# One-core kernel of gated convolution and routed FFN: z is no longer transposed on TensorE in the convolution, the gates are computed in the FFN, and x's statistics come from two ScalarE passes

## The reference

```python
# convolution; c is the context, both keys and values
x = x + tanh(g_xattn) * conv_attention(k=c, v=c, q=layernorm(x))
#   kv[i, j] = k_i * v_j (8 x 8 products per head and batch); y = causal convolution of kv
#   with the head's filter of 1024 taps, plus D * kv; out_j = sum_i y[i, j] * q_i
z = layernorm(x)                     # 8192 tokens of 1024
# FFN
def ffn(t, w1, w2):                  # w1: 1024 x 1024, w2: 512 x 1024
    a, b = split(t @ w1, 2)
    return (a * silu(b)) @ w2
shared = ffn(z, shared_w1, shared_w2)
aff = sigmoid(z @ gate_w + expert_bias)                 # gate_w: 1024 x 7
mask = two best experts of each token
for e in range(7):
    sel = the 1170 tokens with the best where(mask, aff, -1) for e
    routed[sel] += ffn(z[sel], w1[e], w2[e]) * where(mask, aff, 0)
out = x + tanh(g_ffn) * (shared + routed)
```

## Time and profile before

| what | value |
|---|---|
| time, three runs | 4091.8 us median (4090.35 to 4098.31) |
| profiled execution | 4100.51 us, of which the span is 4098.7 us |
| mean granted clock of TensorE | 0.997 |
| TensorE busy | 4040.9 us, 99% of the span |
| VectorE, ScalarE, GpSimd busy | 2575.6, 1953.6 and 1455.2 us |
| DMA traffic | 632.27 MB |

### The profile page before, as it was taken

The page is one execution under the profiler, slowest core; times in us unless marked ns, Lnnn a source line. Parts: engine busy times, 40 slices in busy tenths (PEclk is TensorE's granted clock), DMA queues, the critical chain, the costliest instruction groups (busy, mean ns, idle before and its releaser), DMA issues.

```text
span 4098.7 us, 71212 instructions
## 1 busy us (share of the span) xinstructions
PE 4040.9 (99%) x25370; PEld 3679.4 (90%) x25370; DVE 2575.6 (63%) x3032; ACT 1953.6 (48%) x2601; POOL 1455.2 (36%) x1465
## 2 busy tenths in 40 slices
PE   8999999999999999999999999999999999999999
PEld 7999999999999999998788777888888988988887
DVE  8999999999999999998443432222334433434342
ACT  7888888888888888885111111111122121212120
POOL 2444444444444444441000024443214434334341
PEclk9999999999999999999999999999999999999999
DMA  7888888888888888886223233433444545545443
GB/s 190 224 217 222 216 223 219 220 216 223 220 219 220 219 221 218 221 213 200 85 85 101 86 100 100 107 90 98 117 120 109 105 94 115 100 99 115 79 99 49
DMA packets 267383, 632.27 MB, mean 154 GB/s; under 512 B 32890, under 2 KB 99162, under 8 KB 267256
## 3 DMA queue, kind: packets, MB, share of 16 engines
q1 hardware_dynamic: 206376, 414.05, 32.8%
q0 software_dynamic: 60880, 216.44, 29.4%
HBM read 311.44 MB, written 170.16 MB: 117 GB/s over the span
## 4 chain that ended last, share of the span: by engine, by line
PE 48%; DVE 1%; DMA 1%; issue 1%; POOL 1%; ACT 0%; SPq 0%; POOLq 0%; DVEq 0%; PEldq 0%; ACTq 0%
PE mem_acc L2031 11%; PE mem_acc L2032 11%; PE mem_acc L2033 11%; PE moe_ps L2050 3%; PE moe_ps L2051 3%; PE moe_ps L2052 3%; PE moe_psT L2052 2%; PE moe_psT L2051 2%; PE moe_psT L2050 2%; POOL moe_zin L1591 0%; DMA out<-moe_y 0%; DVE moe_zl L1917 0%; DMA moe_ranks<-z_d,moe_get_i 0%; DMA moe_y<-out 0%; DMA moe_zin<-z_d,moe_get_i 0%
## 5 line engine op out<-in xcount | busy, mean ns | idle before, releaser
L2031 PE MATMUL mem_acc<-moe_zh,moe_w1h 128*128 128x512 f32 (+2 forms) x2336 | 849.5, 364 | 16.2 <-issue 6.9
L2032 PE MATMUL mem_acc<-moe_zl,moe_w1h 128*128 128x512 f32 (+2 forms) x2336 | 845.8, 362 | 0.0
L2033 PE MATMUL mem_acc<-moe_zh,moe_w1l 128*128 128x512 f32 (+2 forms) x2336 | 845.5, 362 | 0.0
L909 PE MATMUL mem_acc<-att_kv_hi,att_tz_hi 128*128 128x288 f32 x2560 | 768.5, 300 | 19.9 <-DVE att_pick L848 18.0
L911 PE MATMUL mem_acc<-att_kv_hi,att_tz_lo 128*128 128x288 f32 x2560 | 757.0, 296 | 0.0
L910 PE MATMUL mem_acc<-att_kv_lo,att_tz_hi 128*128 128x288 f32 x2560 | 756.9, 296 | 0.0
L1940 DVE TENSOR_TENSOR moe_hid<-mem_acc,moe_act_s 128x512 f32<-128x512 f32 (+2 forms) x148 | 91.5, 618 | 758.5 <-PE mem_acc L2033 610.5
L909 PEld LDWEIGHTS mem_acc<-att_kv_hi,att_tz_hi 128*128 128x128 f32 x2560 | 482.5, 188 | 32.0 <-DVE att_pick L848 18.0
L2031 PEld LDWEIGHTS mem_acc<-moe_zh,moe_w1h 128*128 128x128 f32 x2336 | 442.5, 189 | 75.9 <-issue 19.3
L2033 PEld LDWEIGHTS mem_acc<-moe_zh,moe_w1l 128*128 128x128 f32 x2336 | 442.3, 189 | 56.9
L2032 PEld LDWEIGHTS mem_acc<-moe_zl,moe_w1h 128*128 128x128 f32 x2336 | 442.7, 190 | 56.0 <-issue 0.2
(11 more groups left out here) (235 smaller groups left out, 8668.7 us busy)
## 6 DMA issues: line engine op xcount, KB each, us to landing
att_kv_lo<-att_kv POOLq DMA_DIRECT2D x126, 1152.0 KB, 9.7
att_kT<-in_cT SPq DMA_DIRECT2D x64, 512.0 KB, 6.5
att_xn<-in_x SPq DMA_DIRECT2D x64, 512.0 KB, 8.3
out<-att_x SPq DMA_DIRECT2D x64, 512.0 KB, 7.2
z_d<-att_z SPq DMA_DIRECT2D x64, 512.0 KB, 5.9
zT_d<-att_zT SPq DMA_DIRECT2D x64, 512.0 KB, 8.5
moe_y<-out SPq DMA_DIRECT2D x128, 256.0 KB, 4.3
out<-moe_y SPq DMA_DIRECT2D x128, 256.0 KB, 5.1
```

What stands on the lines that cost most here:

```text
L909: nc.tensor.matmul(acc, w_hi[:, cols], x_hi, start=start, stop=False, skip_group_check=True)
L2031: nc.tensor.matmul(acc, w1h[j][:, c, b, :], zh[:, c, 0:w], start=(c == 0), stop=False)
L2032: nc.tensor.matmul(acc, w1h[j][:, c, b, :], zl[:, c, 0:w], start=False, stop=False)
L2033: last = nc.tensor.matmul(acc, w1l[j][:, c, b, :], zh[:, c, 0:w], start=False, stop=(c == C - 1))
```

## The change

- The convolution no longer transposes z, stores zT, or computes gates and logits. `turn_z`, `gates`, `sum_gates`, `columns`, `gate_parts`, `logits` and `store_zT` go. z is stored by four transfers per head, which exchange blocks of columns so that a row holds the features of its token in another order; VectorE's 32 x 32 transposes then bring a loaded tile into the form that the products need, and the rows of w1 and of the gate weights are loaded in the matching order.
- x's mean and variance come from two passes of ScalarE with an accumulated sum, `sum_x` and `squares_x`, which write to PSUM (`unread`, two banks, where psZ and psL were). GpSimd makes the negative mean between them.
- In the FFN VectorE transposes each shared tile (`turn_shared`). Tiles 0 and 1 are turned ahead of the last column block, the others inside the window.
- The gates are computed in shared groups 1 to 5: 32 batches of two tiles. GpSimd loads a pair of tiles (1 MB), VectorE turns it (`turn_pair`), TensorE makes eight products of 256 columns and two sums, ScalarE evicts the parts, VectorE adds the bias. The full-array blocks stand before and behind each batch.
- The scores are made in group 6, the routing steps follow with nine per group, so that LEAD is 11. The lists are scattered without staging copies, and seven VectorE steps (`codes`) turn token numbers into rows of the new order.

```diff
-    z_rows = z_d[0:B * S, :].rearrange("(b h j) l -> h b j l", b=B, j=HD)
+    QD = L // 4
+    z_rows = [bass.AP(z_d.tensor, q * (P // 4 * L), [[P * L, H], [QD, 4], [L, P // 4], [1, QD]]) for q in range(4)]
...
-                sp.dma_start(z_rows[h], z[:, :]).then_inc(z_out, 16)
-
-            def store_zT(h):
...
+                for q in range(4):
+                    sp.dma_start(z_rows[q][h], z[:, q * QD:(q + 1) * QD]).then_inc(z_out, 16)
...
+                sp.dma_start(mem.first_z[t], z_tiles[t]).then_inc(ffn_z_in[t], 16)
...
-                if back2:
-                    store_zT(h - 2)
...
+                pool.wait_ge(x_summed, h + 1)
+                wait(pool, x_squared, h)
+                pool.sem_inc(passed, 1)
+                nc.gpsimd.tensor_scalar(minus_mean_x[:, :], x_sum[:, :], -1.0 / L, None, ALU.mult).then_inc(x_centered, 1)
...
+                link(nc.gpsimd.tensor_scalar(root[0][:, 0:1], x_square[:, :], 1.0 / L, EPS, ALU.mult, ALU.add), 1)
...
+            def sum_x(h, u):
+
+                act.wait_ge(x_in[u], uses(h, u))
+                wait(act, x_centered, h)
+                nc.scalar.activation(unread[:, :], xn[u][:, :], ACT.Identity, accum_out=x_sum[:, 0:1]).then_inc(x_summed, 1)
+
+            def squares_x(h, u):
+
+                act.wait_ge(x_centered, h + 1)
+                wait(act, rooted[0], ROOT * h)
+                nc.scalar.activation(unread[:, :], xn[u][:, :], ACT.Square, bias=minus_mean_x[:, 0:1], scale=1.0,
+                                     accum_out=x_square[:, 0:1]).then_inc(x_squared, 1)
...
                 more = not (isinstance(h, int) and h >= H - 2)
+                sum_x(h, u)
                 if back2:
                     normal_x1(h - 2)
                 if ahead:
                     squares(h + 1, 0)
                 conv_out(h, 0)
+                squares_x(h, u)
                 conv_out(h, 1)
                 if ahead:
                     high(h + 1, 1 - u, 0)
-                if back2:
-                    columns(h - 2, 0)
                 conv_out(h, 2)
...
-                if back2:
-                    columns(h - 2, 1)
...
-                if back2:
-                    gate_parts(h - 2)
...
+            def ffn_z_turn(t):
+
+                dve.wait_ge(ffn_z_in[t], 16)
+                nc.vector.transpose(mem.first_z[t], mem.first_z[t]).then_inc(ffn_z_turned, 1)
...
@@ -864,19 +835,21 @@
                 if ahead:
                     pairs(h + 1, 1)
                 else:
+                    ffn_z_turn(0)
+                    ffn_z_turn(1)
                     ffn_z_low(0)
...
                 if not ahead:
+                    ffn_z_turn(2)
+                    ffn_z_turn(3)
...
-                if back2:
-                    logits(h - 2)
...
-            def gates(h):
...
-                last.then_inc(parts_done, 1)
-
...
-                nc.tensor.matmul(psL[:, L_AT:L_AT + E], part_s[:, :], pick[:, :], start=True, stop=True).then_inc(l_done, 1)
-
...
-                    if back2:
-                        sum_gates(h - 2)
...
-                if back2:
-                    turn_z(h - 2, 0)
...
-                if back2:
-                    turn_z(h - 2, 1)
...
-                if back2:
-                    gates(h - 2)
...
         STEPS = list(range(BITS)) + ["compare", "scan ties", "scan ties on", "keep", "scan kept", "scan kept on",
                                      "number", "first", "second", "weigh", "no second", "no first"]
-        EACH = 2 * (FC - 1)
-        PLACES = [["scores"]] + [STEPS[a:a + EACH] for a in range(0, len(STEPS), EACH)] + [[]]
+        EACH = 3 * (FC - 1)
+        GATED = 5
+        PLACES = [["setup"]] + [[] for _ in range(GATED)] + [STEPS[a:a + EACH] for a in range(0, len(STEPS), EACH)]
         LEAD = len(PLACES)
-        assert LEAD == 9 and GS >= LEAD + 3 and (GS - 1 - LEAD) % 2 == 0
+
+        def gate_slots(k):
+
+            if not isinstance(k, int) or not 1 <= k <= GATED:
+                return {}
+            places = [(j, b) for j in range(FC) for b in (1, 0)]
+            places = places[4:] if k == 1 else places[:7]
+            start = 0 if k == 1 else 4 + 7 * (k - 2)
+            return {place: start + n for n, place in enumerate(places)}
...
+            def load_pair_of_tiles(n, half):
+
+                wait(pool, parts_done, n - 1)
+                for i in range(2):
+                    pool.dma_start(halves_of_raw[half][:, i * D:(i + 1) * D], z_tiles[2 * n + i]).then_inc(pair_in[half], 16)
+
+            pool.wait_ge(zh_set, 2 * GT)
+            pool.wait_ge(zl_set, 2 * GT)
+            pool.wait_ge(w2h_set, FC)
+            pool.wait_ge(w2l_set, FC)
+            load_pair_of_tiles(0, 0)
+            load_pair_of_tiles(1, 1)
+            with pool.Fori(1, BATCHES // 2) as n:
+                load_pair_of_tiles(2 * n, 0)
+                load_pair_of_tiles(2 * n + 1, 1)
...
-            def scatter_column(h):
-
+            for h in range(H):
                 for n in range(2):
...
+                    nc.gpsimd.indirect_dma_start(list_of[n], bass.IndirectOffsetOnAxis(slot_of[:, h, n:n + 1], 0),
+                                                 pay[:, h, n, :], None).then_inc(scattered[n], 16)
...
-                nc.scalar.activation(zh[:, :, cols], place_of(grp, t).rearrange("p (c n) -> p c n", c=C),
+                act.wait_ge(z_turned, grp.tile + (t + 1))
+                nc.scalar.activation(by_token(zh, t, 0, QUARTERS), by_quarter(place_of(grp, t), QUARTERS),
                                      ACT.Copy).then_inc(zh_set, 1)
...
+                act.wait_ge(parts_done, n + 1)
...
+                nc.scalar.activation(part_s, psP, ACT.Copy).then_inc(parts_set, 1)
...
+            def make_scores():
+
+                dve.wait_ge(parts_done, BATCHES)
...
-                nc.vector.tensor_tensor(zl[:, :, cols], place_of(grp, t).rearrange("p (c n) -> p c n", c=C),
-                                        zh[:, :, cols].bitcast(F32), ALU.subtract).then_inc(zl_set, 1)
+                nc.vector.tensor_tensor(by_token(zl, t, 0, QUARTERS), by_quarter(place_of(grp, t), QUARTERS),
...
+            def turn_pair(n):
+
+                dve.wait_ge(pair_in[n % 2], 32 * (n // 2) + 32)
+                nc.vector.transpose(halves_of_raw[n % 2], halves_of_raw[n % 2]).then_inc(pair_turned, 1)
...
+            def turn_ahead(gating, j):
+
+                for b in (1, 0):
+                    if (j, b) in gating:
+                        n = gating[j, b]
+                        turn_pair(n)
+                        if n > 1:
+                            logits(n - 2)
...
+            def codes():
+
+                dve.wait_ge(merged, 5)
...
+                a, b = code[:, 0, :], code[:, 1, :]
+                link(v.tensor_scalar(a, tokens[:, :], 6, 0x7E00, ALU.logical_shift_left, ALU.bitwise_and), 1)
+                link(v.tensor_scalar(b, tokens[:, :], 4, 0x60, ALU.logical_shift_right, ALU.bitwise_and), 2)
...
+                link(v.tensor_tensor(a, a, b, ALU.bitwise_or), 7)
+                v.tensor_copy(merged_at[:, :], a).then_inc(coded, 1)
...
+            def turn_shared(grp, t):
...
+                nc.vector.transpose(place_of(grp, t), place_of(grp, t)).then_inc(z_turned, 1)
...
-                quartered = nxt is not None and nxt.kind == "routed"
+                gating = gate_slots(cur.k) if cur.kind == "shared" else {}
+                if cur.kind == "shared" and isinstance(cur.k, int) and cur.k == GATED + 1:
+                    make_scores()
+                if cur.kind == "shared" and isinstance(cur.k, int) and cur.k == GS - 1:
+                    codes()
+                turn_ahead(gating, 0)
...
+                    turn_ahead(gating, j + 1)
...
-                        for step in places[2 * j:2 * j + 2]:
+                        for step in places[3 * j:3 * j + 3]:
...
+                if BATCHES - 1 in gating.values():
+                    logits(BATCHES - 2)
+                    logits(BATCHES - 1)
+                if nxt is not None:
+                    for t in range(nxt.nt) if prev is None else range(2, early_tiles(nxt)):
+                        turn(nxt, t)
...
+            def gates(n):
...
+                    q = c % 4
+                    z = halves_of_raw[n % 2].rearrange("p (g c n) -> p c g n", c=C, n=SQ)[:, c]
+                    last = nc.tensor.matmul(psT[q * GQ:(q + 1) * GQ, 0, 0:2 * P], gate_q[:, c, :], z,
+                                            start=(c < 4), stop=(c >= C - 4))
+                last.then_inc(parts_done, 1)
...
+            def sum_gates(n):
...
+                    last = nc.tensor.matmul(psS[:, i, 0:E], part_s[:, i * P:(i + 1) * P], pick[:, :], start=True, stop=True)
+                last.then_inc(sums_done, 1)
...
+                        elif places and j > 0 and b == 0 and prev is not None:
+                            first_product(cur, j, b, 0, C // 2)
+                            if left:
```

(10 more changed lines are left out.)

316 lines of the change are left out of this document (142 added, 174 removed).

## The result

The changed kernel takes 4170.5 us (median of four runs, 4163.2 to 4173.2) against 4091.1 us for the one before: the ratio estimated from all runs is 1.0189, with a 95% interval of 1.0177 to 1.0201. The forecast was slower by 29.5 us; it is slower by 79.5. The profiled execution after has 4169.9 us and a span of 4168.2, so the two profiles differ by 69.5 us.

What follows compares the result with a forecast made beforehand. TensorE's queue was taken to bound the kernel. Convolution -33.5 (112.2 gained less 78.7 of waits), passage +3, gates +46, windows +12, routing +2 gave +29.5 on 4091.8, about 4121 us; range 4080 to 4170.

Steps and rivals of the forecast that it cites:

- part 2: Convolution, ScalarE's two added passes: first output late, TensorE waits 1.29 us a head, 78.7 us; bounds -6 to +12.
- Rival A: Convolution: ScalarE is in time at the head's start, the whole 112 us is gained, 4042 us; chance 0.12.
- the threshold it was given: Convolution: if `conv(h, 2)` waits less than 0.81 us a head, the change is no longer slower.
- The rest of the head I followed in the same way: Convolution behind the first output: later outputs, sign changes, queries, statistics and transfers make no further wait; taken as 0.
- part 1: Convolution: TensorE loses z transposes, gate products and the sum of parts, 1.84 us a head, 112.2 us gained.
- part 4: Shared FFN groups: 32 gate batches at 1.44 us on TensorE, +46 us; no wait for loads.
- rival C: Gate products in shared groups: column strips don't overlap at this width, 4198 us; chance 0.03.
- Rival B: Gate batches in shared groups: pair loads come late, +44 us, 4165 us; chance 0.10.
- part 5: Ten FFN windows: VectorE's transposes delay result 4, half 6 waits 1.2 us; +12 us, between 0 and 25.
- part 6: Routing from group 6: scores delay the first count, +2 us; third count and code steps 0; bound 0 to +10.
- I give it no price of its own: TensorE's clock stays at the 2.4 GHz level; a drop was named as a risk but given no separate cost.
- part 3: Passage from convolution to FFN: four tile transposes enter VectorE's nearly full queue; +3 us, between 0 and +7.

Runs made afterwards that it cites:

- The square: Kernels before and after, each with x's statistics on VectorE or ScalarE; a head takes 29.25 or 30.26 us before, 27.88 or 29.06 after.
- the run with z later: Kernel after with statistics on VectorE, new window order, tiles 0 and 1 transposed earlier, and x1 normalised behind output 0: 4074.1 us, ratio 0.9959.
- The run with four parts: Kernel after with statistics on VectorE, new window order, earlier tile transposes, and last-head queries ahead of the tiles' high parts: 4081.3 us, ratio 0.9978.

## Why the prediction was right and wrong

**Right: the order of ScalarE's queue decides (part 2).** The wait at `conv(h, 2)` was forecast at 1.29 us and is 1.18; the sum pass without a bias took 1.04 us, not 1.13. Moving the sum removed it, and that alone was worth 62 to 63 us; it must be moved into idle time, though, as behind output 0 it made the fifth block wait instead. Rival A fell, since ScalarE was late. So did the threshold it was given (no slower below 0.81 us a head): with that wait gone the kernel is still 17 us slower than before, because the other terms are larger than forecast.

**Wrong: "The rest of the head I followed in the same way ... I take 0 for all of this" (part 2).** This is the step that failed, by 21 us: the largest of the misses, on a term that was put at nothing. The outputs and sign changes come late at two more blocks, 0.19 and 0.26 us a head, 27 us in all, against 7 us that the first wait was shorter. Seen from part 1 it is the same loss, not a further one: the 1.84 us are what the removed products occupy, but some stood where TensorE would otherwise have waited for ScalarE. The square shows 1.37 and 1.20 us as their worth. I had the z group ahead of the third block in the sum, and treated the one before the fifth and the sum of parts ahead of the seventh as pure gain. Of the 0.47 us that 1.37 lacks of 1.84, the run with z later shows 0.16 to be the queue's order again; 0.26 is the break at the seventh block, which is still there (distances of 0.29 and 0.24 us on average). In that run's trace ScalarE works without a pause from TensorE's second x group through the queries, the high part and output 5 to the sign change, so its queue sets this one too; no run tried it.

**The gates (part 4)** were mis-sized by the sums: 0.44 us for two, not 0.28, 5 us in all. The wait of 2.40 us at the last sums was in no term. The bound by strips side by side held to 0.01 us, so rival C fell. The Trainium skill ("TensorE: Matmul & The Clock Gate", on column tiling) says that column strips run at the same time; the trace agrees at this width too. Rival B fell: the load took 4.5 us, and TensorE's waits name no batch. It is the right kind of bound to fear, but the row of 9.7 us was of an adding transfer at the fullest time of the kernel.

**The windows (part 5)** came out near the forecast: 9.9 us for the transposes (nine windows at 23.47 us and the first at 23.22, against the 224.5 of the kernel before without its stall), where 12 was said. Its own upper bound was not needed.

**Wrong: the third count "I take as 0" (part 6).** It costs nothing as a count (some 0.23 us of TensorE each, as before). But with nine in a group the last one ends just behind the last block, and what stands behind it on VectorE, two transposes, moves into the window: 5.3, 4.3 and 4.1 us behind groups 6 to 8, 13.7 in all, of which 8.2 are waits and the rest is the clock. The bound I gave was 10. The run with the transposes one block earlier gave 12.0 of it back.

**Wrong: the clock, "I give it no price of its own".** In the convolution it did hold: 1.00 from 600 to 1100 us, with a wait in every head. But TensorE does stop in the shared groups, and 1.3 us is not longer than any wait there: the trace of the kernel before has one of 4.00 us, behind which a product takes 0.80 us instead of 0.39, at a clock of 0.94 over the window:

```profile
2428.89 0.80 PE L2050 MATMUL moe_ps<-moe_w2h,moe_hh 128*128 128x512 f32 x1 [4.00 <-DVE moe_y L1954]
```

After, the clock costs 7.9 us in the windows behind groups 5 to 8, and some 3 more in the passage than before. What decides is not shown: the same wait of 2.82 us was followed by the lower clock in the kernel after and not in the run with the gates twice.

**The passage (part 3)** cost 7.7 us, just outside 0 to 7. About 3 of it are the clock, which is 0.91 from 1865 to 1960 us and was 0.95. The tiles land, are transposed and only then rounded, and the queries stand behind them in ScalarE's queue, after:

```profile
1867.46 1.06 ACT L599 ACTIVATE moe_zh<-moe_zin 128x1024 fp32r<-128x1024 f32 x1 [2.42 <-DVE moe_zin L771]
1870.15 1.06 ACT L599 ACTIVATE moe_zh<-moe_zin 128x1024 fp32r<-128x1024 f32 x1 [1.63 <-DVE moe_zin L771]
```

The run with four parts showed that taking the queries out of there gives nothing back, so what costs the other 4 or 5 us stays open.

On ScalarE's destination, the sum took 1.024 us on average to PSUM in the kernel after and 1.056 to SBUF in the run on the kernel before: 0.03 us. The Trainium skill ("ScalarE: Activation LUTs", the remark on writing PSUM) has the direction right; for two passes that is 0.06 us of ScalarE's time a head.

## What to carry to other kernels

Work that is moved to an engine with idle time is costed at its place in that engine's queue, and for the whole period: after the first wait is found, go on to the next hand-over, and the next. Work that is removed from the bounding engine gives only what no wait fills; ask at each removed instruction when the one behind it could have started. And a step that is put last before a hand-over (a ninth count, a transpose) delays all that stands behind it by its full length, while the same instruction a place earlier cost a fraction. A stall can cost more than its length: read the granted clock of the stretch behind it. And before a difference of a few us is explained from one profile, see how far that execution lies from its kernel's median, and look at the same stretch in a second profile.

## What the runs showed of the hardware

A GpSimd instruction on one column took 0.25 us at one place and 2.28 at another, where it began 0.09 us after a VectorE product of two SBUF tiles and ended as that ended. The Trainium skill ("SBUF — State Buffer", on the two separate sides) describes an exclusive port pair of the two engines, held for a whole instruction; these rows agree with it, and the run in which ScalarE made the mean took 112 us off the kernel with that order. That it was the port and nothing else was not tried apart.

At TensorE's lower clock the full-array products of 512 columns start 0.43 us apart instead of 0.23. Among the shared groups it was granted behind waits of 2.40 to 4.00 us, and one wait of 2.82 us passed without it: the same window took 28.78 us with it and 26.33 without.

The last thing is small: two sums of 7 columns between full-array blocks took 0.44 us, as much as a group of four 128-column transposes.
